# Where the last four tiles of an expert phase are scaled: next to their own bias instead of one tile later

## The reference

```
x = x + 0.5 * ffn(layernorm(x))
x = x + attn(layernorm(x))
x = x + 0.5 * ffn(layernorm(x))

ffn:  probs = softmax(x @ w_gate + b_gate)          # 8 experts
      route_p, route_idx = max(probs), argmax(probs)
      y[e] = relu(x @ W1[e] + b1[e]) @ W2[e] + b2[e]  # 128 -> 512 -> 128
      out = y[route_idx] * route_p
```

## Time and profile before

| what | value |
|---|---|
| time, median of three runs (lowest, highest) | 322.14 us (321.22, 323.71) |
| span of the profiled execution, first to last instruction | 319.3 us |
| median less that span | 2.8 us |
| PE busy | 276.5 us, 87% |
| DVE busy | 214.5 us, 67% |
| POOL busy | 178.8 us, 56% |
| expert phase 0: DVE's first and last scale start | 47.0 and 86.4 us |
| expert phase 1: POOL's first and last scatter start | 270.9 and 311.6 us |

### The profile page before, as it was taken

One profiled execution on the slowest core, in us unless ns is written; L12 is line 12 of the kernel. 1 busy time (PEld: TensorE's weight loads), 2 busy tenths in 40 slices (PEclk: granted clock), 3 DMA queues, 4 the chain that ended last, 5 costly groups with the idle time before them and its releaser, 6 DMA issues.

```text
span 319.3 us, 7990 instructions
## 1 busy us (share of the span) xinstructions
PE 276.5 (87%) x2396; PEld 224.1 (70%) x2396; DVE 214.5 (67%) x691; ACT 159.7 (50%) x389; POOL 178.8 (56%) x319
## 2 busy tenths in 40 slices
PE   8573999999995776999999999998977699999960
PEld 8463999999994363656666566665646588999960
DVE  3877048788608759987666777776787555888850
ACT  2430076666204834586666667768541107666620
POOL 5577815554525201587777787788657730554551
PEclk9855999999999998799999999999976579999996
DMA  6973141220040731662524522110001143222100
GB/s 180 403 293 119 53 95 54 65 63 31 24 126 8 199 121 53 197 180 88 156 79 134 152 72 74 57 53 6 3 19 42 42 121 86 51 67 71 34 10 0
DMA packets 34387, 29.37 MB, mean 92 GB/s; under 512 B 4108, under 2 KB 28817, under 8 KB 34352
## 3 DMA queue, kind: packets, MB, share of 16 engines
q1 hardware_dynamic: 29696, 23.52, 24.6%
q0 software_dynamic: 2496, 4.27, 4.1%
q10 hardware_dynamic: 2160, 1.14, 1.4%
HBM read 17.08 MB, written 12.55 MB: 93 GB/s over the span
## 4 chain that ended last, share of the span: by engine, by line
PE 58%; POOL 11%; DVE 10%; issue 7%; DMA 5%; ACT 4%; POOLq 1%; ACTq 0%; SPq 0%; DVEq 0%
PE bank L1279 13%; PE bank L1290 12%; PE bank L1207 5%; PE bank L1436 3%; PE bank L1408 3%; PE bank L1384 3%; POOL pT L541 2%; POOL row L454 2%; PE bank L1381 2%; PE bank L1414 2%; PE bank L1271 2%; POOL disp_d L462 2%; PE bank L1240 2%; PE bank L1466 2%; PE bank L1389 1%
## 5 line engine op out<-in xcount | busy, mean ns | idle before, releaser
L723 ACT ACTIVATE pT<-bank 128x512 f32<-128x512 f32 x96 | 56.4, 599 | 36.2 <-PE bank L1414 25.2
L1207 PE MATMUL bank<-zero 128*128 128x128 f32 x298 | 43.2, 314 | 9.4 <-DVE rowi L916 4.7
L1279 PE MATMUL bank<-xsT,ew 128*128 128x128 f32 x368 | 48.8, 276 | 0.2
L1290 PE MATMUL bank<-experts,hT 128*128 x368 | 48.9, 276 | 0.0
L1207 PEld LDWEIGHTS bank<-zero 128*128 128x128 f32 x298 | 41.6, 227 | 10.1 <-DVE rowi L916 4.7
L1038 DVE TENSOR_REDUCE mh<-bank 128x2 f32<-128x512 f32 x64 | 42.1, 682 | 8.5 <-PE bank L1384 8.2
L541 POOL TENSOR_SCALAR_AFFINE_SELECT pT<-pT 128x512 f32<-128x512 f32 x62 | 39.8, 643 | 10.2 <-ACT pT L723 9.9
L1279 PEld LDWEIGHTS bank<-xsT,ew 128*128 128x128 f32 x368 | 44.7, 192 | 0.7 <-ACT xsT L621 0.3
L1290 PEld LDWEIGHTS bank<-experts,hT 128*128 128x128 f32 x368 | 44.8, 192 | 0.5 <-issue 0.3
L627 ACT ACTIVATE hT<-bank,ew 128x128 f32<-128x128 f32 x92 | 28.8, 364 | 28.9 <-PE bank L1279 28.9
L923 DVE TENSOR_SCALAR hT<-bank,ew 128x128 f32<-128x128 f32 x92 | 28.0, 346 | 20.2 <-PE bank L1279 18.9
(11 more groups left out here) (133 smaller groups left out, 479.4 us busy)
## 6 DMA issues: line engine op xcount, KB each, us to landing
sp_d<-spl SPq DMA_DIRECT2D x32, 192.0 KB, 2.6
experts<-in_experts SPq DMA_DIRECT2D x8, 578.0 KB
qz<-sp_d SPq DMA_DIRECT2D x32, 96.0 KB
ks<-sp_d SPq DMA_DIRECT2D x32, 96.0 KB
xs_sb<-disp_d SPq DMA_DIRECT2D x46, 66.0 KB, 1.8
row<-in_x SPq DMA_DIRECT2D x4, 256.0 KB, 5.5
row<-x_d SPq DMA_DIRECT2D x4, 256.0 KB, 5.0
disp_d<-pad ACTq DMA_DIRECT2D x12, 66.0 KB, 2.3
```

Source lines behind the costliest of these rows:

```text
L723: act.activation(pT[:, u, :], bank[2 + u % 2][:, :], ACT.Exp, scale=SCALE).then_inc(a_e, 1)
L1207: pe.matmul(bank[b][:, 0:P], zero[:, :], zero[:, :], start=True, stop=True)
L1279: mm = pe.matmul(bank[2 + 2 * (k % 2) + c // 2][:, (c % 2) * P:(c % 2 + 1) * P], ew[:, k % WRING, c * P:(c + 1) * P], xsT[:, k % 2, :], st ...
L1290: mm = pe.matmul(bank[6 + k % 2][:, 0:D], hT[:, k % 2, c, :], w2.rearrange("p a c -> p (a c)"), start=(c == 0), stop=(c == HC - 1))
```

## The change

Two conditions of the loop are changed. Up to t = 19 the loop is as before. At t = 19, 20, 21 and 22 the tile's own scale is called after its bias (at t = 19 after weights(22), too), and the scale of the tile before is no longer called at t = 20 and 21.

```diff
                     bias(t)
-                    if 0 < t < NS - 1:
+                    if 0 < t <= NS - 4:
                         scale(t - 1)
                     if t + WRING < NS:
                         if (t + WRING) % 4 == 0:
                             te_ = loaded(mybir.EngineType.DVE, te[0:1, t + WRING:min(t + WRING + 4, NS)], NE - 1)
                         weights(t + WRING, t % WRING)
-                    if t >= NS - 2:
+                    if t >= NS - 4:
                         scale(t)
```

## The result

The changed kernel takes 319.91 us (median of 16 runs, 318.47 to 321.25) where the kernel before takes 321.88 us beside it (16 runs, 319.73 to 323.80). The ratio is 0.9929, with a 95% interval from 0.9909 to 0.995: 0.7% faster, 2.3 us of 322 (1.6 to 2.9); the two medians alone lie 1.97 us apart. It was measured twice more beside the experiments, at 0.9902 (0.987 to 0.9935) and 0.9925 (0.9895 to 0.9956). The ratios are those of the fast runs: a few that lie apart are left out, the furthest one of 403.58 us, at a mean granted clock of 0.63, with the new order in phase 1 alone.

What follows compares the result with a forecast made beforehand. Each phase's end was taken as bound by its last scatter, delayed by POOL's 1.28 us pitch. Gains of 1.17 and 1.18 us sum to 2.35: 322.14 - 2.35 = 319.8 us, range 318.4 to 321.8.

Steps and rivals of the forecast that it cites:

- The last scatter sets what follows: At both phase ends, tile 22's scatter sets the reload or the drain; gains 1.17 and 1.18 us.
- a drain that runs from its own issue: Rival, end of phase 1: POOL's drain does not follow the last scatter, so no gain there; 321.0 us, 13 in 100.
- an attention stage that gives phase 0's gain back: Rival, after phase 0: a wait not hanging on the reload cancels that gain; 321.0 us, 7 in 100.
- The durations of the sum: Phase ends: scale start to scatter 1.13 us, scatter to scatter 1.28, bias to its own scale 0.32.
- The cover: Scales of tiles 19 and 20 fit DVE's idle time before relu(21) and relu(22), ending 0.06 and 0.24 us before them.
- A scale that must wait out a running scatter: Rival, phase ends: scale(20) is blocked by tile 19's scatter, making the kernel slower; 322.5 us, 4 in 100.
- The median: Whole kernel: median forecast 319.8 us, keeping its 2.84 us distance above the profiled span, predicted as 316.95.
- TensorE's clock: Rival, attention stage: low-clock stretch 4 us longer gives 321.8 us (8 in 100), 4 us shorter 317.8 (6 in 100).

Runs made afterwards that it cites:

- phase 1 alone: New order of the last scales in expert phase 1 only, old order in phase 0, against the kernel before: ratio 0.9973 (0.9939 to 1.0007).
- last three tiles: Both bounds NS - 3 instead of NS - 4, so tile 19's scale goes back behind bias(20); against the kernel before: 0.9967 (0.9938 to 0.9996).
- two behind: Scale runs two tiles behind bias, yb has three buffers, tiles 20 to 22 scaled after the last bias; against the kernel before: 1.0076 (1.0044 to 1.0107).
- phase 0 alone: New order of the last scales in expert phase 0 only, old order in phase 1, against the kernel before: ratio 0.9963 (0.9933 to 0.9993).
- the change again: The unaltered changed kernel, rerun in the two later comparisons against the kernel before: ratios 0.9902 (0.987 to 0.9935) and 0.9925 (0.9895 to 0.9956).

## Why the prediction was right

*The last scatter sets what follows.* Right, at both ends: the reload starts 0.14 us after the landing, and POOL's drain became shorter by 1.16 us although it starts where it did, relative to scale(22). The rival of a drain that runs from its own issue falls with the 7806 and 7807 ns of the profiles above: in all thirteen profiles the drain ends 6.45 us after the last scatter's end, be it 7.8, 8.5 (last three tiles), 9.0 or 9.3 us (two behind) long. The rival of an attention stage that gives phase 0's gain back is less firmly excluded, by the time of phase 0 alone. The phases by themselves, from the first hidden record on PE to the start of the last scatter:

| kernel | phase 0 | phase 1 | scale(22) to its scatter |
|---|---|---|---|
| before | 47.20 | 47.23 | 2.45, 2.46 |
| the change | 46.11 | 45.98 | 1.29, 1.30 |
| the change again | 45.88 | 46.18 | 1.29, 1.30 |
| phase 0 alone | 46.04 | 47.18 | 1.29, 2.46 |
| phase 1 alone | 47.26 | 46.03 | 2.45, 1.31 |
| last three tiles | 46.73 | 46.70 | 1.95, 1.96 |
| two behind | 48.59 | 48.48 | 3.59, 3.34 |

*The durations of the sum.* 1.28 us from scatter to scatter and 1.13 from scale to scatter held; so did the 0.32 us from a bias to its own scale (0.32 to 0.33 at all three tiles). The Trainium skill's rule that the semaphore costs nothing (*VectorE: DVE Perf Modes*, "The DRAIN you can't avoid") is therefore not what these rows show, 0.21 against 0.33. One duration was 0.08 us off: scale(19) begins 0.41 us after weights(22), not 0.49 (82.04 to 82.45), which gives more room before relu(21). The trace of before already has this distance, between other copies and the relu behind them (0.41 us, seven times), where DVE need not wait. In phase 0 the distances of the last scatters came as 1.29, 1.28, 1.65 and 1.29 us against 1.28, 1.28, 1.59 and 1.28; in phase 1 as 1.28, 1.35, 1.42 and 1.28, against 1.28, 1.28, 1.58 and 1.28; the 1.35 has a scatter of 1.04 us in it (last section), which did not reach the end because tile 21's scatter waits for its scale. The gain of each phase was 1.16 us instead of 1.17 and 1.18.

*The cover.* Both moved scales fit in front of the relus, with 0.20 and 0.22 us left in phase 0. In phase 1 relu(21) shows no idle time in front of it, and it starts as long before bias(20) as it did (0.89 us) and together with ACT's half (304.63), so PE's release still decides.

*A scale that must wait out a running scatter.* scale(20) at 84.21 begins 0.02 us after tile 19's scatter and takes its 0.35 us. The rival falls, and by more than this pair: 397 scales in the thirteen profiles began inside a running scatter, and every one took 0.34 or 0.35 us. The blocking that the Trainium skill states in *SBUF — State Buffer*, "Who interferes with whom", is therefore not seen in this order. In the other order, a scatter that begins inside a scale or a weights copy, rows do show a wait of its kind (first point of the last section).

*The median.* 319.8 was forecast against 319.91, but this closeness is partly luck: the predicted span was 316.95 and the profiled one 317.7. The sum of the two gains, -2.32, is in it; the rest is phase 0's later last scale (+0.76, 86.36 to 87.12, of which 0.69 is the filler above). What made up for it is the 2.84 us between span and median that were taken as kept. They are not a cost of the kernel: where the record has an execution's time and its span, the two lie 1.7 to 1.8 us apart, so some 1.1 us of the 2.84 only say that the profiled execution of before was quicker than the median one. With the change the same distance came out as 2.2 us. The base moved as well, from 322.14 (3 runs) to 321.88 (16 runs). Between the last scatter of phase 0 and scale(22) of phase 1 the two executions took the same time, 220.35 us (88.81 to 309.16, 88.41 to 308.76), a reload that is 0.31 us shorter and a rest that is as much longer; the other profiles have 217.5 to 224.0 us there, so this agreement is chance.

*TensorE's clock* was a rival with a price of about 2 us to either side. The low stretches did fall elsewhere in each profile, and their cost is visible in front of phase 0. The runs show how far time and clock go together: over the 71 executions of the kernel before that were run beside the experiments, the time falls by 1.4 us for each 0.01 of mean granted clock (correlation -0.78). The change's runs that enter the ratios of the two later comparisons had 0.911 and 0.908 where those of before had 0.906 and 0.905. By that slope, an estimate, 0.8 and 0.5 us of the 3.0 and 2.5 us between their means go with the clock; 2.3 and 2.0 us are left, near the 2.32 of the two ends. In the same way phase 0 alone is left with a gain of 1.3 us, phase 1 alone with 1.4, the last three tiles with 1.2, and two tiles behind with a loss of 2.3. This is a correlation: whether the change itself brings more clock or chance did is not shown.

## What to carry to other kernels

Where a stage ends in a queue with a fixed pitch (here 1.28 us for a scatter), read the idle time in front of its last few entries: a delay at the first of them reaches the end where the entries behind it follow at the pitch. So an order that costs nothing in the steady part, such as a step that runs one tile behind, can cost time there even if the last entry's own producer is not late. Bring the producers of the last entries forward only as far as the next bound allows; going on to all tiles gave nothing. When an effect is smaller than the spread of whole executions, read it as a distance between two rows that lie close together, and use single-part kernels to see whether the distances add up to the time.

## What the runs showed that was not expected

- A scatter can be held up by DVE. With every tile next to its own bias, a scatter began 0.22 us after a weights copy (DVE, then POOL) and took 1.12 us instead of 0.98:

```profile
303.25 0.49 DVE L931 TENSOR_SCALAR ew<-experts 128x644 f32 x1 [0.56 <-issue]
303.47 1.12 POOL L470 DMA_INDIRECT out<-ys_sb,xs_sb  x1 [0.92 <-DVE ys_sb L947]
```

The 29 scatters of all profiles that began with 0.16 to 0.29 us of such a copy or of a scale still to run ended 0.85 to 0.86 us after that instruction's end, and so took 1.01 to 1.15 us; the one at 306.01, begun inside scale(20) (305.85 to 306.20), is one of them. The 330 that began with 0.16 us or more of a relu to run, which reads PSUM, took 0.98 to 1.00. Where a scatter begins only 0.05 to 0.08 us after a scale, it is the scale that is longer, 0.37 to 0.40 us in four cases (in the kernel with phase 1 alone 0.40 at 304.50, with a scatter begun at 304.57). None of this set an end here.

- The reload of the rows is fickle: from the last scatter to the first statistics on DVE it took 6.4 to 7.4 us in most profiles and 5.0 to 5.2 us in three, in kernels that do not touch it; in those three the first of the four loads landed 2.7 to 2.9 us after its start, elsewhere 4.1 to 5.1.
- The attention stage, from its first transpose to the first hidden record of phase 1, took 164.4 to 169.0 us in profiles of kernels that share its code. That spread is more than the whole effect studied here.
